# Output projection of a four-head-group attention: plain fp32 products replaced by three fp32r passes

## What is computed

```python
# q: 16 heads of 96 columns, in 4 groups of 4 heads; each group shares one key and value head (KV = 4)
hidden = concatenate([context, latents], axis=1)
k = (hidden @ Wk.T); v = (hidden @ Wv.T); q = latents @ Wq.T
scores = einsum('bkgqd,bksd->bkgqs', q, k) / sqrt(96)
out = einsum('bkgqs,bksd->bkgqd', softmax(scores), v)
out = out.reshape(b, q_len, 16 * 96)
x = x + tanh(g_xattn[1]) * (out @ Wo.T)          # 1536 x 512 output projection
```

## Time and profile before

| | |
|---|---|
| median of three runs | 1615.02 us (1611.8 to 1615.87) |
| profiled execution, device time | 1614.25 us |
| profiled execution, span | 1612.5 us |
| TensorE busy | 1570.8 us, 97% |
| VectorE, ScalarE, GpSimd busy | 977.4, 741.2, 399.8 us |
| x1 stage, first pair starts / last ends | 892.6 / 1253.4 us of the span |
| granted TensorE clock, mean | 0.997 |

### The profile page before, as it was taken

How to read it: one execution, slowest core, us unless ns; L and a number is a source line. 1 busy time by engine, 2 the same in 40 slices (tenths; PEclk the granted TensorE clock), 3 DMA queues, 4 the chain that set the end, 5 groups by cost and what they waited for, 6 DMA issues and landing times.

```text
span 1612.5 us, 25907 instructions
## 1 busy us (share of the span) xinstructions
PE 1570.8 (97%) x8958; PEld 1262.4 (78%) x8958; DVE 977.4 (61%) x2629; ACT 741.2 (46%) x2151; POOL 399.8 (25%) x278
## 2 busy tenths in 40 slices
PE   8999999999999999999999999999999999999987
PEld 7788888888888888888885877868696788666556
DVE  6762663626636356364686774848476767756677
ACT  5442443424434344243432462735355332288873
POOL 3131321313203132032203300000001343377651
PEclk9999999999999999999999999999999999999999
DMA  5110111101111011111224000000001613000001
GB/s 180 53 43 30 56 42 52 42 29 55 42 52 42 29 55 42 39 43 43 79 80 195 14 1 14 0 13 0 0 1 41 223 53 108 14 14 15 1 1 53
DMA packets 34435, 76.22 MB, mean 47 GB/s; under 512 B 5568, under 2 KB 18496, under 8 KB 32192
## 3 DMA queue, kind: packets, MB, share of 16 engines
q1 hardware_dynamic: 34368, 75.36, 14.0%
HBM read 73.25 MB, written 2.10 MB: 47 GB/s over the span
## 4 chain that ended last, share of the span: by engine, by line
PE 78%; DVE 11%; ACT 4%; issue 3%; DVEq 2%; POOL 1%; DMA 1%; POOLq 0%; SPq 0%; ACTq 0%
PE banks L1197 10%; PE banks L1142 10%; PE banks L1115 10%; PE banks L1123 9%; PE banks L1357 9%; PE banks L1461 5%; PE banks L1254 3%; PE banks L1237 3%; PE banks L1433 3%; PE banks L1244 2%; ACT p L992 2%; PE banks L1564 1%; PE banks L1571 1%; PE banks L1587 1%; PE banks L1381 1%
## 5 line engine op out<-in xcount | busy, mean ns | idle before, releaser
L1197 PE MATMUL banks<-w_o,atT 128*128 128x512 f32 x720 | 181.0, 397 | 0.0
L535 POOL TENSOR_TENSOR w_q<-w_raw_q,w_q 128x1792 fp32r<-128x1792 f32 x15 | 61.1, 4072 | 479.6 <-ACT w_q L741 479.6
L1115 PE MATMUL banks<-cT,w_k 128*128 128x512 f32 x720 | 178.0, 396 | 0.0
L1142 PE MATMUL banks<-w_v,cT 128*128 128x512 f32 x768 | 176.5, 390 | 0.0
L1142 PEld LDWEIGHTS banks<-w_v,cT 128*128 128x128 f32 x768 | 144.0, 188 | 29.7
L1123 PE MATMUL banks<-xT,w_q 128*128 128x512 f32 x672 | 164.0, 395 | 0.7 <-ACT kT L731 0.7
L1898 DVE TENSOR_TENSOR sA<-banks,pbias 128x512 f32<-128x512 f32 x62 | 42.8, 690 | 186.5 <-PE banks L1237 185.7
L1115 PEld LDWEIGHTS banks<-cT,w_k 128*128 128x128 f32 x720 | 132.0, 188 | 25.4
L1197 PEld LDWEIGHTS banks<-w_o,atT 128*128 128x128 f32 x720 | 131.8, 188 | 25.4
L1123 PEld LDWEIGHTS banks<-xT,w_q 128*128 128x128 f32 x672 | 123.8, 188 | 26.0 <-ACT kT L731 1.1
L800 ACT ACTIVATE sA<-sA,nmA 128x128 f32<-128x128 f32 x248 | 96.4, 393 | 55.8 <-DVE nmA L1903 55.5
(11 more groups left out here) (291 smaller groups left out, 3275.3 us busy)
## 6 DMA issues: line engine op xcount, KB each, us to landing
w_raw_v<-in_w0v SPq DMA_DIRECT2D x8, 1024.0 KB, 4.8
w_raw_q<-in_w0q SPq DMA_DIRECT2D x16, 512.0 KB, 3.3
w_raw_k<-in_w0k SPq DMA_DIRECT2D x15, 512.0 KB, 3.4
w_raw_o<-in_w0o SPq DMA_DIRECT2D x15, 512.0 KB, 3.3
cTp<-in_ctxT SPq DMA_DIRECT2D x12, 512.0 KB, 3.9
wq_raw<-in_wq SPq DMA_DIRECT2D x1, 3072.0 KB, 10.0
wo<-in_wo SPq DMA_DIRECT2D x1, 3072.0 KB, 20.3
x_res<-in_x SPq DMA_DIRECT2D x4, 512.0 KB, 11.4
```

Source lines behind the costliest of these rows:

```text
L535: pool.tensor_tensor(w_part[slot][1][:], w_raw[slot][:], w_part[slot][0][:].bitcast(F32), ALU.subtract).then_inc(S(f"w{slot}_lo"), 1)
L1115: mm = pe.matmul(dst, wk_[l][:, c, h * P:(h + 1) * P], cT[r][:, c, half * HT:(half + 1) * HT], start=c == 0 and n == 0, stop=c == DC - 1 a ...
L1142: mm = pe.matmul(dst, cT[l][:, c, b * P:(b + 1) * P], wv_[r][:, c, :], start=n == 0, stop=n == 3 * DC - 1)
L1197: mm = pe.matmul(dst, at_at(l, p, b // 4 * 2 + h)[:, t], w[r][:, h, :], start=start and n == 0, stop=stop and n == 5)
```

## The change

`project` becomes three fp32r passes. `wo1` and the attended rows `at1` get a high and a low part each, held for two key heads at a time (slot kv % 2); the raw values share their place with the low part. The projection of key heads 0 and 1 is summed in a bank and added to `x_res` (`add_out`) within kv = 2, that of 2 and 3 at the end of the pair. SyncE loads `wo1` in quarters, four per pair: those of kv = 2 and 3 after the projections of 0 and 1 (`x1_out`), those of the next pair after the pair's last, each after the one before has landed. ScalarE splits them (`out_high`, three copies of 128x512) ahead of kv = 0 and within kv = 2 and 3; GpSimd makes the low parts (`out_rest`). ScalarE now takes all attended rows out of the banks, waits for its own writes (drain) and makes the high part (128x384); GpSimd subtracts (`split_attended`). VectorE's copies for b = 0 are gone. The queries of group 3 move on TensorE behind the turns of kv = 2, since they use the banks of the projection. Semaphores are renamed (`w1_hi`, `w1_lo`, `const_ready`).

```diff
@@ tiles
-        wo1 = sb(ctx_1, "wo1", [P, NCH * KV1, D])
+
+        wo1, wo1_raw = [], []
+        for k in range(2):
+            high_1 = sb(ctx_1, f"wo1_0_{k}", [P, NCH, D], F32R)
+            ctx_x = ExitStack()
+            wo1_raw.append(sb(ctx_x, f"wo1_raw_{k}", [P, NCH, D]))
+            ctx_x.close()
+            wo1.append([high_1, sb(ctx_1, f"wo1_1_{k}", [P, NCH, D], F32R)])
         q1 = sb(ctx_1, "q1", [HD1, 2, G1, PT2], F32R)
-        at1 = sb(ctx_1, "at1", [P, NCH * KV1, PT2])
+        at1_hi = sb(ctx_1, "at1_0", [P, 2 * NCH, PT2], F32R)
+        ctx_x = ExitStack()
+        at1_raw = sb(ctx_x, "at1_raw", [P, 2 * NCH, PT2])
+        ctx_x.close()
+        at1 = [at1_hi, sb(ctx_1, "at1_1", [P, 2 * NCH, PT2], F32R)]
         p1 = sb(ctx_1, "p1", [P, 2, G1, 2 * P])
         k1 = sb(ctx_1, "k1", [HD1, KV1, 2, 2 * P], F32R)
         v1 = sb(ctx_1, "v1", [P, 2, 2, KV1 * HD1], F32R)
...
@@ block.sync
-            sp.dma_start(wo1[:], A["wo1"]).then_inc(S("wo1_ld"), 16)
+            def out_weights(n, kv):
+
+                if not (isinstance(n, int) and n == 0):
+                    sp.wait_ge(S("wo1_ld"), 16 * n)
+                sp.dma_start(wo1_raw[kv % 2][:], A["wo1"][:, NCH * kv:NCH * (kv + 1), :]).then_inc(S("wo1_ld"), 16)
+
+            out_weights(0, 0)
+            out_weights(1, 1)
...
-            with sp.Fori(1, NPAIR) as i:
-                next_ctx(i, i)
+            def second_out_weights(i):
+                sp.wait_ge(S("x1_out"), 4 * i + 2)
+                out_weights(KV1 * i + 2, 2)
+                out_weights(KV1 * i + 3, 3)
+
+            def next_out_weights(i):
+                sp.wait_ge(S("x1_out"), 4 * i + 4)
+                out_weights(KV1 * i + 4, 0)
+                out_weights(KV1 * i + 5, 1)
+
+            next_ctx(1, 1)
+            for i in range(NPAIR - 2):
+                second_out_weights(i)
+                next_out_weights(i)
+                next_ctx(i + 2, i + 2)
+            second_out_weights(NPAIR - 2)
+            next_out_weights(NPAIR - 2)
+            second_out_weights(NPAIR - 1)
             sp.wait_ge(S("x1_s"), NB * KV1)
             load_ffn("f1")
...
@@ block.gpsimd
-                pool.wait_ge(S("wq1_hi"), kv + 1)
+                pool.wait_ge(S("w1_hi"), kv + 1)
...
+            def out_rest(i, kv):
+                for c in range(NCH):
+                    pool.wait_ge(S("w1_hi"), KV1 + NCH * (KV1 * i + kv) + c + 1)
+                    pool.tensor_tensor(wo1[kv % 2][1][:, c, :], wo1_raw[kv % 2][:, c, :],
+                                       wo1[kv % 2][0][:, c, :].bitcast(F32), ALU.subtract).then_inc(S("w1_lo"), 1)
+
+            def split_attended(i, kv, b):
+                k, t = slice(NCH * (kv % 2), NCH * (kv % 2) + NCH), slice(b * P, (b + 1) * P)
+                pool.wait_ge(S("x1_ah"), 2 * (8 * i + 2 * kv + b) + 2)
+                pool.tensor_tensor(at1[1][:, k, t], at1_raw[:, k, t], at1[0][:, k, t].bitcast(F32),
+                                   ALU.subtract).then_inc(S("x1_at"), 1)
+
             def x1_pool(i, last):
                 rsqrt(NPAIR * (L1X - 1) + i + 1)
+                out_rest(i, 0)
+                out_rest(i, 1)
+                for kv in range(KV1):
+                    if kv == 2:
+                        out_rest(i, 2)
+                    if kv == 3:
+                        out_rest(i, 3)
+                    for b in range(2):
+                        split_attended(i, kv, b)
                 if not last:
                     context_rest(i + 1)
             pairs_ahead(pool, x1_pool)
...
@@ block.scalar, x1_act
+                def out_high(kv):
+                    act.wait_ge(S("wo1_ld"), 16 * (KV1 * i + kv + 1))
+                    for c in range(NCH):
+                        act.activation(wo1[kv % 2][0][:, c, :], wo1_raw[kv % 2][:, c, :], ACT.Copy)\
+                           .then_inc(S("w1_hi"), 1)
+
                 queries(0, 0, 2)
                 queries(0, 2, NCH)
-                def attended(kv, b):
-                    act.wait_ge(S("x1_pv"), 8 * i + 2 * kv + b + 1)
+                out_high(0)
+                out_high(1)
+
+                def attended(kv, b, heads=True, rest=True):
                     src, t = bank(2 + 2 * b).rearrange("p (h t) -> p h t", h=G1), slice(b * P, (b + 1) * P)
-                    act.activation(at1[0:HD1, NCH * kv:NCH * kv + NCH, t], src[0:HD1, 0:NCH], ACT.Copy)
-                    if b == 1:
+                    c0 = NCH * (kv % 2)
+                    if heads:
+                        act.wait_ge(S("x1_pv"), 8 * i + 2 * kv + b + 1)
+                        act.activation(at1_raw[0:HD1, c0:c0 + NCH, t], src[0:HD1, 0:NCH], ACT.Copy)
+                    if rest:
                         for c in range(NCH):
-                            e = act.activation(at1[HD1:P, NCH * kv + c, t], src[c * BLK:(c + 1) * BLK, G1 - 1], ACT.Copy)
-                        e.then_inc(S("x1_at1"), 1)
+                            e = act.activation(at1_raw[HD1:P, c0 + c, t], src[c * BLK:(c + 1) * BLK, G1 - 1], ACT.Copy)
+                        e.then_inc(S("x1_ah"), 1)
+                        act.drain()
+                        act.activation(at1[0][:, c0:c0 + NCH, t], at1_raw[:, c0:c0 + NCH, t], ACT.Copy).then_inc(S("x1_ah"), 1)
 
                 for kv in range(KV1):
+                    more = kv + 1 < KV1
                     probs(kv, 0)
                     probs(kv, 1)
-                    for b in range(2):
-                        probsT(kv, b)
-                        if kv + 1 < KV1:
-                            queries(kv + 1, 2 * b, min(2 * b + 2, NCH))
-                        attended(kv, b)
+                    probsT(kv, 0)
+                    if more:
+                        queries(kv + 1, 0, 2)
+                    if kv >= 2:
+                        out_high(kv)
+                    attended(kv, 0, rest=False)
+                    probsT(kv, 1)
+                    attended(kv, 0, heads=False)
+                    if more:
+                        queries(kv + 1, 2, NCH)
+                    attended(kv, 1)
...
@@ block.tensor, x1_pe
-                pe.wait_ge(S("wq1_lo"), 1)
+                pe.wait_ge(S("w1_lo"), 1)
...
+                        if h == 0 and kv > 0:
+                            pe.wait_ge(S("x1_ah"), 2 * (8 * i + 2 * kv + b) - 3)
...
-                def project(b, n0, n1):
-                    for n in range(n0, n1):
-                        mm = pe.matmul(bank(6 + b), at1[:, n, b * P:(b + 1) * P], wo1[:, n, :], start=n == 0,
-                                       stop=n == NCH * KV1 - 1)
-                    if n1 == NCH * KV1:
+                def project(kv, b, c0=0, c1=NCH):
+
+                    pe.wait_ge(S("x1_at"), 8 * i + 2 * kv + b + 1)
+                    pe.wait_ge(S("w1_lo"), KV1 + NCH * (KV1 * i + kv + 1))
+                    if kv == 2 and c0 == 0:
+                        pe.wait_ge(S("q1_lo"), 8 * i + 8)
+                    k = kv % 2
+                    for c in range(c0, c1):
+                        for n, (l, r) in enumerate(PASSES):
+                            mm = pe.matmul(bank(6 + b), at1[l][:, NCH * k + c, b * P:(b + 1) * P], wo1[k][r][:, c, :],
+                                           start=k == 0 and c == 0 and n == 0,
+                                           stop=k == 1 and c == NCH - 1 and n == len(PASSES) - 1)
+                    if k == 1:
                         mm.then_inc(S("x1_out"), 1)
 
                 for kv in range(KV1):
+                    more = kv + 1 < KV1
                     for b in range(2):
                         if kv == 0:
                             pe.wait_ge(S("v1_ready"), 4 * i + 3 + b)
-                        else:
-                            pe.wait_ge(S(f"x1_at{b}"), 4 * i + kv)
                         scores(kv, b)
-                    more = kv + 1 < KV1
-                    if more:
-                        pe.wait_ge(S("wq1_lo"), kv + 2)
+                        if kv == 1 and b == 0:
+                            pe.wait_ge(S("w1_lo"), kv + 2)
+                            queries(kv + 1, 0, 1, 0, 2)
+                        if kv == 2:
+                            project(0, b)
+                            project(1, b)
+                        if kv == 3 and b == 0:
+                            project(2, 0, 0, 2)
+                    if kv == 0:
+                        pe.wait_ge(S("w1_lo"), kv + 2)
                         queries(kv + 1, 0, 2)
                         queries(kv + 1, 2, NCH, 0, 1)
-                    else:
-                        pe.wait_ge(S("wo1_ld"), 16)
-                        project(0, 0, 2 * NCH - 1)
+                    if kv == 1:
+                        queries(kv + 1, 0, 1, 2, DC)
+                        queries(kv + 1, 1, 2)
+                        queries(kv + 1, 2, NCH, 0, 1)
+                    if kv == 3:
+                        project(2, 0, 2, NCH)
+                        project(2, 1, 0, 1)
```

(63 more changed lines are left out.)

## The result

The changed kernel takes 1620.19 us, the kernel before 1614.79 us (medians of five runs each). The ratio is 1.0041, 95% interval 1.0029 to 1.0052: 5.4 us slower, where 4.1 were forecast. The profiled execution has a span of 1618.5 us, 6.0 more than before. Two executions further down, one of e2 (7537.76 us) and one of e4 (3121.33 us), stand far above all others of the same kernels and are left out of every median and ratio here.

A forecast was written before the change was run, and what follows sets the result against it. TensorE was taken to set the stage; its 4.3 us gain per pair goes to hand-overs. 1614.25 + 1.2 (four pairs) + 2.9 (last wait) = 1618.35, or 1619.1 in terms of the median; range 1608 to 1625.

The forecast's parts named there:

- VectorE's removed copies buy nothing: Key heads 0 and 1: removing copies (0.89 us) and the 0.5 us wait moves the next scores' end at most 0.1.
- T: In kv = 2, the moment the projection of key heads 0 and 1 is done, forecast at 1043.0 in pair 1.
- The turn of kv = 3: Key head 3: turn possible 5.7 us after T+12.2, TensorE has work for 4.1, so 1.6 us lost.
- U: The moment the turn of kv = 3 is possible, forecast at T+17.9.
- The tail: End of a pair, after U: project(3, 0) starts at U+7.5, 1.4 us late; the pair ends at U+12.5.
- +0.3 per pair: Net change of each pair of x1, with a few semaphore waits: +1.2 us for four; bounds -1.1 to +1.7 per pair.
- The last pair: End of x1: TensorE waits for GpSimd's split of the next block's weights, +2.9 us.
- Columns decide: Rival, x1: hand-overs shorter than summed, so the 4.3 us gain per pair stays in part; 1606 us, chance 0.15.
- Late load: Rival, kv = 2: weight load lands after T+5.2; with 7.5 us, 2.3 per pair, 1628 us; chance 0.08.
- the tail stays hidden: Rival, end of x1: ScalarE is earlier than summed; 1616 us, chance 0.10.
- The 8 us of waits per pair: TensorE's summed waits per pair in the new order, for a stage that had 2; weighed in favour of columns deciding.
- The tiles' port: Rival, pair's tail: VectorE's xn scaling goes first, GpSimd's split_attended(3, 0) waits 0.5 to 1.0 us; 1621 to 1623, chance 0.17.

The follow-up runs named there:

- e2: Changed kernel with ScalarE's drain and high part of the b = 0 attended rows moved behind the third query block's copy: 1614.88 us, ratio 1.0011 to the kernel before.
- e4: Changed kernel with TensorE's wait for the split feed-forward weights moved to the first base product: 1618.42 us, ratio 1.0033 to the kernel before.
- e6: Changed kernel without streaming the second half of the weights; key heads 2 and 3 reuse those of 0 and 1: 1614.47 us, ratio 1.0005 to the kernel before.
- e7: Changed kernel as it is, timed on another chip: 1622.38 us, ratio 1.0051 to the kernel before.
- e10: The kernel of e4 once more, one execution for its rows: span 1618.0 us.
- e1: Changed kernel with one pass (high x high) instead of three in the projection: 1599.51 us, ratio 0.9915 to the kernel before.
- e8: Changed kernel with the moves of e2, e3 and e4, last projection pieces' low-part pass last, feed-forward weights split in four: 1602.15 us, ratio 0.9922 to the kernel before.
- e3: Changed kernel with the two scores of kv = 1 and of kv = 3 next to each other on TensorE: 1613.09 us, ratio 0.9999 to the kernel before.
- e9: The kernel of e2 once more, one execution for its rows: 1613.59 us.

## Why the prediction was right, step by step

- **Sign and size.** 4.1 us slower forecast, 5.4 measured, inside the forecast's own range. TensorE's passes: 16.3 us per pair forecast from 0.227. They run at 0.228 and 0.229 in the two pieces of eighteen, at 0.233 in a piece of six, 0.24 in those of nine and 0.26 in those of three, about 16.9 us per pair if the second piece of six is like the first: cut into short pieces the passes cost 0.6 more than in one long row, and the sum has no term for that.
- **VectorE's removed copies buy nothing.** Shown: no wait for them is left, and the scores wait 0.7 to 1.1 us for the query's low part instead. e2 settles the cause of most of these waits: with one copy of ScalarE moved they fall from 10.7 to 2.5 us.
- **Key heads 1 and 2.** The turn of kv = 1 was to come half a microsecond late; it waits 0.46. T was forecast at 1043.0; pair 1 starts 1.02 us later in the changed kernel, and the turn begins at 1043.95, so 1042.93.
- **From T to the scores of kv = 3.** The second half was to end at T+12.2. It starts at T+11.70, and what follows it at T+12.52. The load was to be hidden and is. The sum has `out_high` with its full 1.6 us, and e6 shows 1.64; only the expectation of e6, written later, made it 0.9. The waits of this stretch are 0.48 and 1.12, where the prediction spoke of over 2 us lost.
- **The turn of kv = 3.** Here the sum was short: U = T+17.9 forecast, T+18.5 measured (1062.46), with a wait of 1.58 for the forecast 1.6. What stands before it (six passes, the second scores, the row maximum, the scaling) took 6.0 for 5.7: 0.1 of the 0.3 is passes and scores (1.40 and 1.45), 0.2 the signal, row maximum and scaling (3.14 for 2.92). The second half of the first scores ended 0.3 later.
- **The tail.** `project(3, 0)` at U+7.5 forecast, U+7.43 measured, wait 1.26 for 1.4. End at U+12.5 forecast, U+12.58 measured.
- **A mis-sized term: +0.3 per pair was 1.0.** Of the 0.7, 0.6 is the turn of kv = 3 above, and 0.17 is the end of the pair before: I took 1073.2 from the edge of the stage in the earlier trace rows, while the first key product starts at 1073.03.
- **How much of the total is luck.** Without the last wait x1 is 4.4 us longer (1.4, 1.0, 0.8 and 1.2 in the four pairs), where four times 0.3 was summed: 3.2 short. The total still came within 1.3 us, since the last wait was 0.4 shorter than forecast, the rest of the program 0.9 shorter in the profiled execution, and the medians lie 5.4 apart where the profiled executions lie 6.0. The order of the waits and their places were right; that the sizes nearly met is in part luck.
- **The last pair.** Forecast 2.9, measured 2.5, and 2.8 in e7. e10 shows that GpSimd's split ends this wait: the base products start 0.09 us behind it.
- **Outside x1** nothing was forecast; the profiled execution is 0.9 us shorter there. That is within the spread: in the profiled executions of this document, with the same work there, x1 starts at 891.93 to 893.93 us, and from the next block's first product to the end it is 358.4 to 360.8 us (359.1 before, 358.6 after).
- **The rivals.** "Columns decide" falls with e1, as does its opposite: half of the columns counted, almost all of them in kv = 2, where the projection stands alone. "Late load" falls, since ScalarE takes the weights up without a gap, and "the tail stays hidden" with the last wait of 2.51 us. The 8 us of waits per pair that the prediction weighs against itself are 6.5. "The tiles' port" occurred in the other order: GpSimd began first (1068.76) and VectorE's two scalings took 1.65 us instead of 0.99, which nobody waited for.

```profile
1068.85 1.65 DVE L1983 TENSOR_SCALAR xn<-x_res,mv,rstd 128x512 f32 x2 [0.79 <-PE banks L1532]
...
1068.76 1.00 POOL L663 TENSOR_TENSOR at<-at_raw,at 128x384 fp32r<-128x384 f32 x1
```

## What to carry to other kernels

A cheaper product on the bounding engine is worth only what the other engines' hand-overs let through: write down the order of each helper engine between two of its results that the bounding engine waits for, and count every instruction in between. Put a helper's new work behind the result on the path, keep two products whose reductions are taken together next to each other, and place a wait at the first instruction that reads the data. Here these moves and the reordered last pieces (e8) turned 0.4 to 0.5% slower into 0.8% faster with the same products.

## What the hardware showed that I had not expected

A wait on TensorE of 2.5 to 2.9 us can cost more than its length, and doesn't always. In e3 a wait of 2.81 us for the feed-forward weights was followed by a granted clock of 0.55 over 3.8 us (1.2 instead of 2.4 GHz for most of it), and the 16 products took 3.79 us; in the changed kernel, after 2.51 us, the clock stayed at 1.00 and they took 2.12.

```profile
1252.60:1256.40 3.80, 3.80 (x17) 3.80 (x18) 2.12 (x2) 0.00 (x0) 2.85 (x3) 0.55 1.03 377
```

In e7 and e9 waits of 2.83 and 2.78 us left it at 1.00 (2.12 us for the same products), in e6 one of 2.87 brought it to 0.58, and in e1 one of 5.05 to 0.50 (3.99 us for them). So of waits of 2.81 and 2.83 us one was followed by the lower clock and one was not: between 2.5 and 2.9 us the length of the wait alone does not tell, and what does is open.
